# Causal maxima, rounding, set-up order and clears of a six-block decoder kernel on one core

## What is computed

```
rel = log(abs(c * rel) + 1.0)
pos_norm = log(abs(c * max(pos, threshold)) + 1.0) + EPS
h = relu((rel / pos_norm)[..., None] * w1[0] + b1)
bias = where(causal, einsum('tsw,wh->hts', h, w2) + b2, -inf)
att = softmax(einsum('bhqd,bhkd->bhqk', q, k) * scale + bias)

act_quant(x) = clip(round(x * scale), -128, 127) / scale,  scale = 127 / max|x| of a token
weight_quant(w) = clip(round(w * scale), -1, 1) / scale,   scale = 1 / mean|w|
```

## Time and profile before

| | |
|---|---|
| median of 3 runs | 3366.53 us (3358.0 to 3366.66) |
| profiled execution | 3359.88 us, span of its instructions 3358.1 us |
[...]
| busy share of the span | PE 88%, PEld 62%, DVE 75%, ACT 65%, POOL 22% |
| read from and written to HBM | 31.24 and 8.39 MB, 12 GB/s over the span |

### The profile page before, as it was taken

How to read it: one execution, slowest core, us unless ns; L and a number is a source line. 1 busy time by engine, 2 the same in 40 slices (tenths; PEclk the granted TensorE clock), 3 DMA queues, 4 the chain that set the end, 5 groups by cost and what they waited for, 6 DMA issues and landing times.

```text
span 3358.1 us, 59674 instructions
## 1 busy us (share of the span) xinstructions
PE 2939.3 (88%) x23279; PEld 2077.8 (62%) x23406; DVE 2527.9 (75%) x5446; ACT 2180.8 (65%) x4271; POOL 753.5 (22%) x1360
## 2 busy tenths in 40 slices
PE   3799986999879998899988998899988998889984
PEld 3556754666656766567655666567665676556763
DVE  6846598756897579975897768976798758887676
ACT  2258763577646876577855777657765677557773
POOL 1420013300232112320133102321032301232000
PEclk8899997999999999999999999999999999999996
DMA  4000010000000000000000000000000000000000
GB/s 154 1 1 1 4 26 16 1 1 5 23 12 9 1 15 12 20 1 1 15 23 9 1 4 16 20 9 1 5 22 15 6 1 15 12 20 1 1 1 13
DMA packets 43467, 43.47 MB, mean 13 GB/s; under 512 B 8576, under 2 KB 41184, under 8 KB 43184
## 3 DMA queue, kind: packets, MB, share of 16 engines
q1 hardware_dynamic: 41200, 36.46, 3.7%
q10 hardware_dynamic: 1984, 3.18, 0.3%
HBM read 31.24 MB, written 8.39 MB: 12 GB/s over the span
## 4 chain that ended last, share of the span: by engine, by line
PE 59%; DVE 23%; ACT 9%; issue 4%; POOL 3%; DMA 1%; SPq 0%; DVEq 0%; POOLq 0%; ACTq 0%
PE banks L1179 9%; PE banks L1212 9%; PE banks L1258 6%; PE banks L1320 4%; PE banks L1221 4%; DVE chain_m L696 4%; PE banks L1197 3%; PE banks L1254 3%; PE banks L1284 3%; DVE chain_arena L890 2%; PE banks L1404 2%; PE banks L1299 2%; DVE chain_arena L774 2%; ACT chain_arena L1013 2%; PE banks L1344 2%
## 5 line engine op out<-in xcount | busy, mean ns | idle before, releaser
L1212 PE MATMUL banks<-chain_arena 64*128 64x256 f32 x3072 | 438.5, 407 | 39.3 <-DVE chain_m L696 28.2
L696 DVE TENSOR_REDUCE chain_m<-banks 128x4 f32<-128x512 f32 x512 | 329.3, 683 | 113.2 <-PE banks L1212 111.5
L1513 POOL TENSOR_SCALAR chain_ng<-chain_sv 128x2 f32<-128x2 f32 x192 | 52.9, 276 | 1448.5 <-DVE chain_sv L677 1448.4
L1212 PEld LDWEIGHTS banks<-chain_arena 64*128 64x128 f32 x3072 | 273.8, 189 | 168.0 <-issue 85.6
L1034 ACT ACTIVATE chain_arena<-chain_arena,chain_m 128x128 f32<-128x128 f32 x1024 | 323.8, 392 | 27.7 <-DVE chain_m L696 25.0
L968 ACT ACTIVATE chain_xn<-chain_xa,chain_nm,chain_rs 128x256 f32<-128x256 f32 x384 | 209.2, 595 | 163.3 <-POOL chain_nm L1517 162.6
L1258 PE MATMUL banks<-chain_arena 64*128 64x256 f32 x2048 | 295.1, 407 | 0.0
L1258 PEld LDWEIGHTS banks<-chain_arena 64*128 64x128 f32 x2048 | 178.7, 188 | 122.7 <-issue 110.6
L692 DVE TENSOR_TENSOR chain_arena<-banks,pos_bias 128x512 f32<-128x512 f32 x256 | 175.1, 684 | 105.4 <-PE banks L1212 105.3
L1221 PE MATMUL banks<-chain_arena,chain_va 128*32 128x128 f32 x5120 | 195.5, 279 | 35.4 <-ACT chain_arena L1013 23.0
L1013 ACT ACTIVATE chain_arena<-banks,chain_mask_k 128x1024 f32<-128x1024 f32 x128 | 142.4, 1113 | 103.3 <-PE banks L1258 102.5
(11 more groups left out here) (314 smaller groups left out, 7013.2 us busy)
## 6 DMA issues: line engine op xcount, KB each, us to landing
chain_xn<-in_ctx SPq DMA_DIRECT2D x32, 256.0 KB, 2.8
chain_xa<-in_x SPq DMA_DIRECT2D x32, 256.0 KB, 3.1
out<-chain_xa SPq DMA_DIRECT2D x32, 256.0 KB, 2.2
chain_arena<-in_mask SPq DMA_DIRECT2D x32, 128.0 KB, 3.7
f_w1t<-in_w1t ACTq DMA_DIRECT2D x1, 1024.0 KB, 7.5
f_w2t<-in_w2t ACTq DMA_DIRECT2D x1, 1024.0 KB, 14.7
wqkv0T<-in_wqkv0T ACTq DMA_DIRECT2D x1, 768.0 KB, 17.1
whh<-in_whh SPq DMA_DIRECT2D x1, 768.0 KB, 10.3
```

Source lines behind the costliest of these rows:

```text
L696: e.tensor_reduce(m, s.rearrange("p (j o) t -> p j o t", o=2), AX.X, ALU.max, negate=True).then_inc(*done(f"{tag}_mx{u}"))
L1212: mm[i] = e.matmul(c.ps[:, i, 2 * T * j:2 * T * j + 2 * T], t["qh"][p, j, x, b, :], flat(t["kx"][p, j, b]), start=not masked, stop=not mas ...
```

## The change

- The causal maxima: the addition and the reduction of a unit become four `tensor_tensor_reduce`, one a head, each of which writes the negated sum of scores and bias (128 x 128) and its minimum, the negated maximum. The Exp reads it with scale -1. The `1_bi` events go.
- The rounding: ScalarE's `g_ro` goes; VectorE adds and subtracts the constant in one instruction.
- Set-up: the division and the Relu are split in halves (16 of the 32 groups each), and the FIRE matmuls with them (`fire_tensor`). On VectorE the slot copies come first, the division stands ahead of the ternary passes of w1t, both ternary weights ahead of c8 to c_cw, conn's softmax behind the position bias, wvo and bvo behind the bias rows. On TensorE the order becomes w1t, first half of FIRE, w2t, conn_t, second half of FIRE, hid_bias, gh, conn, bias rows, wvo, bvo.
- The clears of chains 1 to 3 move into the first GpSimd segment of each.
- All five lists in `ORDER` are new. The chains begin as 0, 2, 3, 1, and chain 1 ends last; the middle of the lists of the four computing engines repeats every second turn. ScalarE's list has 2528 digits where it had 2592, the others are as long as before.

```diff
@@ maxima_vector
-            e.tensor_tensor(flat(t["s"][:, u % 4]), c.ps[:, u % 2, :], flat(k["pos_bias"][:, r]), ALU.add).then_inc(*done(f"{tag}_bi{u}"))
-            e.wait_ge(*dve(f"{tag}_bi{u}"))
-        s = t["s"][:, u % 4] if bias else bank(c, u % 2)
+            for a in range(PER):
+                mx = e.tensor_tensor_reduce(t["s"][:, u % 4, a], bank(c, u % 2)[:, a], k["pos_bias"][:, r, a // 2, a % 2], -1.0, 3e38, ALU.add, ALU.min,
+                                            max_of(t["m"], b, r, a))
+            mx.then_inc(*done(f"{tag}_mx{u}"))
+            yield
+            continue
+        s = bank(c, u % 2)
@@ causal_scalar
-                ex = e.activation(s, s, ACT.Exp, bias=max_of(t["m"], u // GROUPS, row_group(u), a))
+                ex = e.activation(s, s, ACT.Exp, scale=-1.0, bias=max_of(t["m"], u // GROUPS, row_group(u), a))
@@ mlp_vector
-        e.wait_ge(*act(f"g_ro{b}"))
-        e.tensor_scalar(t["hq"][:, :, b, :], cv[:, :, b, :], -ROUND, None, ALU.add).then_inc(*done(f"g_r2{b}"))
+        e.wait_ge(*dve(f"g_mu{b}"))
+        e.tensor_scalar(t["hq"][:, :, b, :], cv[:, :, b, :], ROUND, -ROUND, ALU.add, ALU.add).then_inc(*done(f"g_r2{b}"))
@@ scalar_turn
-    for b in range(B):
-        v = t["cv"][:, :, b, :]
-        e.wait_ge(*dve(f"g_mu{b}"))
-        e.activation(v, v, ACT.Identity, bias=k["rounder"][:, 0:1]).then_inc(*done(f"g_ro{b}"))
-        yield
@@ setup_vector
-    ternary_vector(e, k, ps, ld, su, "w1t", 6)
+    size_vector(e, k, ld, su, "w1t")
+    e.wait_ge(*act("pos_ln"))
+    e.tensor_scalar(pos_n[:], pos_n[:], 1e-6, None, ALU.add).then_inc(*done("pos_eps"))
+    e.wait_ge(*dve("pos_eps"))
+    e.reciprocal(pos_n[:], pos_n[:]).then_inc(*done("pos_rec"))
+    e.wait_ge(*act("rel_ln"))
+    e.wait_ge(*dve("pos_rec"))
+    for i in range(2):
+        part = rel[:, 16 * i:16 * i + 16]
+        e.tensor_tensor(part, part, spread(pos_n[:], 1, 16), ALU.mult).then_inc(*done(f"rel_norm{i}"))
+    ternary_vector(e, k, ps, su, "w1t", 6)
+    size_vector(e, k, ld, su, "w2t")
+    ternary_vector(e, k, ps, su, "w2t", 7)
@@ setup_scalar
-    e.wait_ge(*dve("rel_norm"))
-    e.activation(rel[:], rel[:], ACT.Relu, scale=k["fw1"], bias=k["fb1"]).then_inc(*done("rel_relu"))
+    for i in range(2):
+        part = rel[:, 16 * i:16 * i + 16]
+        e.wait_ge(*dve(f"rel_norm{i}"))
+        e.activation(part, part, ACT.Relu, scale=k["fw1"], bias=k["fb1"]).then_inc(*done(f"rel_relu{i}"))
@@ setup_tensor
     e.matmul(ps[:, 6, 0:1], k["ones"][:], k["a_w1t"][:], start=True, stop=True).then_inc(*done("w1t"))
+    e.wait_ge(*dve("wd3"))
+    fire_tensor(e, k, ps, su, 0)
+    e.wait_ge(*dve("w2t_abs"))
+    e.matmul(ps[:, 7, 0:1], k["ones"][:], k["a_w2t"][:], start=True, stop=True).then_inc(*done("w2t"))
     e.wait_ge(*dve("c_cw"))
     e.matmul(ps[0:H, 5, 0:WIN], k["of_head"], k["conn_cw"][:], start=True, stop=True).then_inc(*done("conn_t"))
...
+    fire_tensor(e, k, ps, su, 1)
...
+def fire_tensor(e, k, ps, su, half):
+    e.wait_ge(*su["act"].of(0)(f"rel_relu{half}"))
+    for s in range(16 * half, 16 * half + 16):
+        mm = e.matmul(ps[:, s // 8, 64 * (s % 8):64 * (s % 8) + 64], k["rel"][:, s, :],
+                      k["fire_w"][:].rearrange("p g h -> p (g h)"), start=True, stop=True)
+        if s % 8 == 7:
+            mm.then_inc(*su["pe"].now(f"fire{s // 8}"))
@@ pool
+def clear(e, c):
+    for tile in ("m3", "fw3"):
+        e.memset(c.t[tile][:], 0.0).then_inc(c.cleared, 1)
+    e.memset(c.t["va"][:], 1.0).then_inc(c.cleared, 1)
+
+def pool_turn(e, c, n, k, first):
+    if n:
+        e.wait_ge(*c.dve.of(n - 1)("y1"))
+    if first:
+        clear(e, c)
...
+            for ch in chains[:EARLY]:
+                clear(e, ch)
+            set_up(e)
+            in_order(ORDER["pool"], lambda c, n: pool_turn(e, chains[c], n, k, n == 0 and c >= EARLY))
```

More of the change, by code:

```diff
@@ L64 @@
     "setup_dve": """
[L65 to L69, removed]
+        wd_zero ones no_bias rel pos_max wd0 wd1 wd2 wd3 c2 bvw0 bvw1 bw10 bw11 bwx0 bwx1 slots slot_mean slotT c4
+        c5 c6 w1t_abs pos_eps pos_rec rel_norm0 rel_norm1 w1t_mean w1t_rec w1t_round w1t_min w1t w2t_abs w2t_mean
+        w2t_rec w2t_round w2t_min w2t c8 c9 c10 c_cw c11 fire_b0 fire_b1 fire_b2 fire_b3 c13 c14 c15 conn_d gate_b
+        half_hn bias1 biasx bias_r0 bias_p0 bias_s0 bias_r1 bias_p1 bias_s1 bias_r2 bias_p2 bias_m0 bias_m1 bias_m2
+        bias3 wvo bvo tau inv_tau""".split(),
     "dve": """
@@ L86 @@
         x_xn0 x_xn1 x_xnT x_q x_k x_v x_mT x_ex0 x_ex1 x_ou0 x_ex2 x_ex3 x_ou1 x_oc g_xn0 g_xn1 g_q1 g_bc g_xqT g_c0
-        g_c1 g_c2 g_c3 g_th0 g_c4 g_c5 g_th1 g_c6 g_c7 g_th2 g_th3 g_ro0 g_ro1""".split(),
+        g_c1 g_c2 g_c3 g_th0 g_c4 g_c5 g_th1 g_c6 g_c7 g_th2 g_th3""".split(),
     "setup_pe": """
-        slot_mean w1t conn_t w2t fire0 fire1 fire2 fire3 conn hid_bias gh wvo bvo bw1 bwx""".split(),
+        slot_mean w1t fire0 fire1 w2t conn_t fire2 fire3 hid_bias gh conn bw1 bwx wvo bvo""".split(),
     "pe": """
@@ L413, in setup_vector @@
                             spread(spread(k["causal"][:, 32 * g:32 * g + 32], 1, 2), 1, GROUPS), ALU.add)
+    e.wait_ge(*act("c_exp"))
+    e.tensor_reduce(cs[:], cw[:], AX.X, ALU.add).then_inc(*done("c13"))
+    e.wait_ge(*dve("c13"))
+    e.reciprocal(cs[:], cs[:]).then_inc(*done("c14"))
+    e.wait_ge(*dve("c14"))
+    e.tensor_scalar(cw[:], cw[:], cs[:, 0:1], None, ALU.mult).then_inc(*done("c15"))
+    e.wait_ge(ld["diag16"], 16)
+    e.wait_ge(*dve("c15"))
+    e.tensor_tensor(dg[:], spread(cw[:], 2, H), k["diag16"][:], ALU.mult).then_inc(*done("conn_d"))
     e.wait_ge(*pe("conn"))
@@ L546, in setup_tensor @@
     mm.then_inc(*done("gh"))
+    e.wait_ge(*dve("conn_d"))
+    e.matmul(ps[:, 5, 16:16 + WIN * H], k["ones"][0:H, :], k["conn_d"][:].rearrange("p a b -> p (a b)"),
+             start=True, stop=True).then_inc(*done("conn"))
+    for i, (tag, w) in enumerate((("1", "wproj"), ("x", "woxT"))):
+        e.wait_ge(ld[w], 16)
+        e.wait_ge(*dve(f"bw{tag}1"))
+        e.wait_ge(*dve("fire_b3"))
+        for j in range(KT):
+            mm = e.matmul(ps[:, 2 + i, 0:D], k["bw" + tag][:, j, :], k[w][:, j, :], start=(j == 0), stop=(j == KT - 1))
+        mm.then_inc(*done("bw" + tag))
     e.wait_ge(ld["wvf"], 16)
@@ L558, in setup_tensor @@
     mm.then_inc(*done("bvo"))
-    for i, (tag, w) in enumerate((("1", "wproj"), ("x", "woxT"))):
-        e.wait_ge(ld[w], 16)
-        e.wait_ge(*dve(f"bw{tag}1"))
-        for j in range(KT):
-            mm = e.matmul(ps[:, 2 + i, 0:D], k["bw" + tag][:, j, :], k[w][:, j, :], start=(j == 0), stop=(j == KT - 1))
-        mm.then_inc(*done("bw" + tag))
+def fire_tensor(e, k, ps, su, half):
[5 more added lines that the diff above has]
+            mm.then_inc(*su["pe"].now(f"fire{s // 8}"))
 def buffers(sb, label):
```

256 lines of the change are left out of this document (110 added, 146 removed).

## The result

The changed kernel takes 3382.02 us (median of 5 executions, 3378.0 to 3382.26), the kernel before, on the same chip, 3366.02 us (3356.91 to 3366.66). The ratio is 1.0055, 95% interval [1.0039, 1.0071]: 0.5% slower, where 1.3% faster was forecast. The profiled execution took 3382.26 us, 3380.5 of them its span.

A forecast was written before the change was run, and what follows sets the result against it. The prediction took the kernel as bound by how tightly the hand-written order packs TensorE against VectorE and ScalarE. Start 3, chain 15 and lists 24 sum to 42 us off: 3318 profiled, 3324 us as median, range 3245 to 3392.

The forecast's parts named there:

- I take a gain of 3 us a turn: All five engine orders: the new lists shorten each of 8 turns by 3 us, 24 us in all.
- the other terms: Start 3 us, and 0.8 us of maxima plus 1.05 us of rounding a turn over 8 turns, 15 us.
- its two ends: Reach of the new lists: from 18 us a turn gained, half the idle time, to 9 us a turn lost.
- Rival (b): New lists lose: 3388 us at 5 us a turn, 3421 at 9; chance 0.12 slower, 0.05 more only eating the gain.
- The fused maxima: Causal units on VectorE: four fused instructions take 1.12 us against 1.32, saving 0.20 us a unit, 6.4 us a turn.
- the lower bound: Four fused maxima on VectorE: 0.84 us, from 0.21 us for a 128x128 two-input instruction without a dependent successor.
- The companion's pitch: Fused maxima on VectorE: 0.07 us added to each instruction, the pitch of MATCH_VALUE_LOAD, the only small companion instruction traced.
- the forecast's chain: Chain of the turn from 2030: the causal addition stands there 4 times, so 0.8 us a turn comes off directly.
- The fused rounding: ScalarE loses 64 instructions of 1149 ns; the removed one is on the turn's chain once, 1.05 us a turn off.
- The set-up: Work before the turns: ends 4 us earlier, at 62.9 us for 66.9; bounds 0 and 8.
- The clears: GpSimd's first segments: chain 1's clear, 2.15 us, precedes the first normalization; 1 us given back, leaving it 3 us earlier.
- The idle time: TensorE idle 36 us in a turn of 396.0; half of it, 18 us, was the lists' largest possible gain.

The follow-up runs named there:

- e1: All edits of the change but with the five old lists, against the kernel before: 3348.58 us, ratio 0.9965.
- e7: All edits with the old lists and the clears back ahead of the turns, against the kernel before: 3341.14 us, ratio 0.9938.
- e6: The changed kernel with its new lists and the clears back ahead of the turns, against the kernel before: 3372.99 us, ratio 1.0034.
- e12: e7 with the second half of the keys left out of the cross attentions' maxima, against the kernel before: 3304.72 us, ratio 0.9828.
- e8: e7 with each ScalarE copy of the transposed probabilities split in four, against the kernel before: 3382.38 us, ratio 1.0056.
- e13: e6 with the second half of the keys left out of the cross attentions' maxima, against the kernel before: 3342.55 us, ratio 0.994.

## Why the prediction was wrong

**The step that failed** is "I take a gain of 3 us a turn" for the lists. Shown, by e1 against after and e7 against e6, is a loss of 33 and 32 us over the run (27 and 30 at equal clock): in e6 against e7 7.6 us a turn in the five middle turns, with some 7 us given back after them. 24 us of gain forecast, 32 of loss found, a difference of 56 us, nearly the whole miss of 58 (3382 - 3324); the other terms, 18 us of gain forecast, came to 13 in e1 (3361.5 beside it - 3348.6), about right in size by luck, since errors cancel (maxima too low, rounding and clears too favourable). The reason given, near zero "because TensorE's own work doesn't shrink" but on the gaining side "with 16 us of VectorE and ScalarE work gone per turn and lists made for the shorter instructions", took what a list is made for as what it does. The measured loss, 32 / 8 = 4 us a turn over the run, lies between its two ends, 18 us a turn of gain and 9 of loss. Rival (b) named the term and the sign; by its own sum 4 us a turn give 3366.5 - 18 + 32 = 3381, and 3382 was measured. It got 0.12. That the new lists repeat only every second turn stood there as the argument for (b), and the turns do alternate, 397 and 413 us; that this is why they are longer no run shows.

**The fused maxima.** The mechanism was right, the price was mis-sized: 1.12 us for four was taken, 0.85 measured, the lower bound (0.84) of the independent neighbour. The companion's pitch (0.07 us for each) was added, where the accumulator's read of 0.08 us in truth runs beside the next instruction (both start at 2258.67). VectorE saves 0.47 us a unit and not 0.20. In the time, 14 us came off with the old lists (8 at equal clock), against the 6.4 (0.8 us x 8) of the forecast's chain. What the chain of one turn showed, 4 units of 32, gives 15 us at 0.47 each (4 x 0.47 x 8): right for the medians, about twice what is left at equal clock.

**The fused rounding.** 1.05 us a turn, 8.4 us in all, was put on the path because it stood on the chain once. Alone it brought nothing: 1.0002 [0.9991, 1.0014], 1.4 us at equal clock. The 64 instructions of 1.15 us go without a trace in the time. A step can stand on the chain that ended last and have others just behind it; that this was so here is the likely reading, not one that was tested.

**The set-up.** Right in the main: it ends 2.8 us earlier for 4 forecast (64.1 for 62.9), and alone it brings 3.3 us. conn_t was indeed what was late next, at 40.94 (39.5 forecast).

**The clears.** The place was right (chain 1, behind chain 3's mask), the price too low: 1 us was taken of the 2.15 that the clears last, and 7 to 9 us came in the medians, 2 to 5 at equal clock. The first normalization is 1.9 us later for it with the new lists (81.28 against 79.43 in e6) and 4.6 us with the old (85.22 in e1 against 80.58 in e7), which accounts for the 2.0 and most of the 5.3 us at equal clock.

**The idle time.** The 36 us a turn of which the prediction took half as the reach of the lists (396.04 - 360.2) rested on a trace that lacks 127 of the 512 matmuls of one line (L1254 before, L1269 after): 127 us of busy time there, 155 us in e12 with all of them, so some 28 us of busy time are missing, 3.5 us a turn, and the idle time is that much less. It decided nothing, but made the possible gain look larger.

## What to carry to other kernels

When a change to instructions comes with a new hand-written order, price the two apart and, before keeping the order, run the new instructions with the old order: here the new instructions under the old order are faster than both (e1, 0.9965 of before, and 0.9938 with the clears ahead). The busy shares did not tell it: e1 and the changed kernel have TensorE at 88%, VectorE at 72% and ScalarE at 63% alike. The one set of lists here that repeats only every second turn alternated between a shorter and a longer turn at every load that was tried; whether that holds for others is open. When two orders of the same work differ, compare the waits line by line, those for loads too, and not only the largest one. And compare granted clocks before reading a difference of a few tenths of a per cent: at 2.3 us for each 0.001, about half of the apparent cost of the clears and of e8 went with it.

## What the runs showed of the hardware that was not expected

- The accumulator's read of a fused instruction (83 ns in its row) adds nothing to the pitch: 0.21 us from start to start for 128x128 float32 from PSUM, as for the cheapest two-input instruction of that size.
- How much of an engine's added work shows in the time depends on the order, and on where the work is added: 42 us added to ScalarE cost 41 us under one set of lists and 7 under another (22 and 8 at equal clock); 136 us taken from VectorE gave 36 and 30, but 120 us added to its causal units under the new lists cost 79 (64 at equal clock).
- The same matmuls took TensorE 21 us longer over five turns under the new lists (e13 against e12), at a granted clock lower by 0.01, while it also idled more: idle time and a lower clock came together.
